# Banded attention: DRAM keeps the operands in token order alone, and the residue order is made on chip

## The reference

```python
x = x + banded_attention(layernorm(x))   # the change is here
x = x + ffn(layernorm(x))
x = x + dense_attention(layernorm(x))
x = x + ffn(layernorm(x))
```

```python
OFFSETS = sorted(set(range(0, 33)) | {48, 64, 96, 128, 192, 256, 384})
scores = stack([einsum('bhnd,bhnd->bhn', q, shift(k, delta)) for delta in OFFSETS]) * scale + pos_bias
alpha  = softmax(scores over the offsets)
out    = sum(alpha[..., i] * shift(v, delta_i))
y      = (out * sigmoid(x @ Wgate + bgate)) @ Wout + bout
```

## Time and profile before

| | us |
|---|---|
| median of 3 runs | 3871.4 (3869.67 to 3877.59) |
| the profiled execution | 3860.39 |
| its span, first to last instruction | 3858.7 |
| of it, groups of the banded attention (186.9 to 1656.6) | 1469.7 |
| TensorE busy / VectorE / ScalarE / POOL, whole span | 2995.9 / 1690.7 / 1363.9 / 494.7 |
| DMA: bytes, whole span | 419.65 MB |
| mean granted TensorE clock | 0.887 |

### The profile page before, as it was taken

The page is one execution under the profiler, slowest core; times in us unless marked ns, Lnnn a source line. Parts: engine busy times, 40 slices in busy tenths (PEclk is TensorE's granted clock), DMA queues, the critical chain, the costliest instruction groups (busy, mean ns, idle before and its releaser), DMA issues. The chain is left out here.

```text
span 3858.7 us, 99901 instructions
## 1 busy us (share of the span) xinstructions
PE 2995.9 (78%) x45340; PEld 1721.1 (45%) x45340; DVE 1690.7 (44%) x2814; ACT 1363.9 (35%) x1358; POOL 494.7 (13%) x395
## 2 busy tenths in 40 slices
PE   0466767686767676768994899989999999997898
PEld 0244545454545454543452344444444444443345
DVE  5123333333333333344044666566566666574302
ACT  0414242433342423123001454445554555554300
POOL 0101020111010111000002121111122121210000
PEclk9678888887888797879976899999999999998896
DMA  5546465645554555422923232222222222212294
GB/s 128 133 84 140 101 148 106 143 103 127 107 141 96 142 103 140 83 98 79 422 115 77 44 70 55 51 50 51 55 59 54 51 59 51 59 34 91 106 421 176
DMA packets 232389, 419.65 MB, mean 109 GB/s; under 512 B 112922, under 2 KB 141412, under 8 KB 215588
## 3 DMA queue, kind: packets, MB, share of 16 engines
q1 hardware_dynamic: 206740, 360.34, 36.5%
q10 hardware_dynamic: 25232, 52.99, 4.5%
HBM read 316.49 MB, written 94.40 MB: 106 GB/s over the span
## 5 line engine op out<-in xcount | busy, mean ns | idle before, releaser
L1353 DVE TENSOR_REDUCE b_tops<-b_slot 128x8 f32<-128x1024 f32 x576 | 680.4, 1220 | 361.6 <-PE b_slot L1210 182.5
L1390 ACT ACTIVATE b_probs<-b_slot 128x1024 f32<-128x1024 f32 x576 | 582.9, 1023 | 550.8 <-PE b_slot L1210 394.9
L1230 PE MATMUL b_outT_ps<-b_probs,b_v 128*17 128x128 f32 (+3 forms) x4608 | 318.1, 384 | 6.2 <-ACT b_probs L1390 5.5
L738 DVE TENSOR_REDUCE a_tops<-a_slot 128x16 f32<-128x1024 f32 x128 | 156.4, 1222 | 362.4 <-PE a_slot L543 361.9
L1210 PE MATMUL b_slot<-b_q_stack,b_k_stack 99*128 99x512 bf16 (+3 forms) x1280 | 274.7, 321 | 43.5 <-DVE b_tops L1353 32.8
L1210 PE MATMUL b_slot<-b_k_stack,b_q_stack 96*128 96x512 bf16 (+3 forms) x1280 | 266.8, 323 | 29.0 <-DVE b_tops L1353 20.1
L780 ACT ACTIVATE a_probs<-a_probs 128x1024 f32<-128x1024 f32 x128 | 133.4, 1053 | 349.3 <-DVE a_probs L729 335.2
L563 PE MATMUL a_slot<-a_bias_q,a_ident 128*128 128x512 bf16 x256 | 96.8, 468 | 196.4 <-DMA a_k_stack<-orders_dram 176.4
L1157 POOL TENSOR_SCALAR_AFFINE_SELECT b_probs<-b_probs 128x1024 f32<-128x1024 f32 x128 | 139.8, 1093 | 809.7 <-ACT b_probs L1390 809.7
L599 PE MATMUL a_outT_ps<-a_probs,a_v_near 128*17 128x64 f32 (+1 forms) x8448 | 147.6, 232 | 87.0 <-issue 84.2
L813 ACT ACTIVATE a_parts<-a_parts 128x1024 bf16<-128x1024 bf16 x96 | 198.1, 2063 | 28.1 <-POOL a_parts L462 14.2
(11 more groups left out here) (217 smaller groups left out, 4328.2 us busy)
## 6 DMA issues: line engine op xcount, KB each, us to landing
f_w_ring<-in_L_ffn_w_dram SPq DMA_DIRECT2D x128, 1024.0 KB, 9.4
orders_dram<-a_parts ACTq DMA_DIRECT2D x96, 512.0 KB
a_k_stack<-orders_dram SPq DMA_DIRECT2D x128, 256.0 KB, 6.7
a_q_stack<-orders_dram SPq DMA_DIRECT2D x64, 384.0 KB, 4.6
parts_dram<-b_parts SPq DMA_DIRECT2D x96, 256.0 KB
a_q_stack<-orders_dram SPq DMA_DIRECT2D x64, 256.0 KB, 5.4
a_k_stack<-orders_dram SPq DMA_DIRECT2D x128, 128.0 KB, 7.6
b_k_stack<-parts_dram SPq DMA_DIRECT2D x64, 256.0 KB, 6.7
```

The costliest lines, as they stand in the source:

```text
L738: ins = dve.tensor_reduce(tops[:, h, :, :].rearrange("p k t -> p (k t)"), src[:, :].rearrange("p (t c) -> p t c", c=64), AX.X, ALU.max)
L1230: ins = pe.matmul(outT_ps[32 * h:32 * h + HD + 1, first:last], v1[b % 2][:, j, HG * g + h, :], src[:, base + first:base + last], start=u = ...
L1353: ins = dve.tensor_reduce(out, src, AX.X, ALU.max)
L1390: act.activation(probs_of(b, g, u, h)[:, :], slot_of(step)[:, :], ACT.Exp).then_inc(taken_act, 1)
```

## The change

- The turns of the parts before the store go. The stores (now behind `part0`, `part1` and as a step `store2`, on ScalarE's queue as before) and `parts_near_dram` hold the token order alone: 256 KB each. The loads are half as large, 7 transfers as before.
- Stacks are split: `q_near`, `k_near` by token, in a ring of 4, and `q_far`, `k_far` by residue, in a ring of 3.
- A new step `turn` per pair makes the residue order from the loaded stack: VectorE for q (2 copies of 96x1024 bf16, one per head), ScalarE for k (2 as well). Both wait for the load and for `S` of the pair three back; `mx` waits for the turn of its head instead of the load.
- Schedule: in a group, loads of pair n + 4 stand behind the second `S` and of pair n + 5 behind `mrow`; the turn of pair n + 3 stands behind the second `S`, the turn of n + 4 ahead of PV. Four pairs are loaded at the start, three turned. A division now pops two steps at a time, `store2` alone.
- `mrow` writes the near and the far stack with a transfer each: 8 per group instead of 4.
- `perm` shrinks to one row of 144 columns, of which eight windows are used.

```diff
     def division(which, b, half):
-        return [(step, b, half, which) for step in ("part0", "rest1", "turn0", "part1", "part2", "turn1", "turn2")]
+        return [(step, b, half, which) for step in ("part0", "rest1", "part1", "part2", "store2")]
...
+    def turned(n):
+
+        return [("turn",) + pair_of(n)] if n < 2 * B * G else []
...
-    first += operands(0) + operands(1) + operands(2) + projection("q", 0, 1) + projection("k", 0, 1)
+    first += operands(0) + operands(1) + operands(2) + operands(3) + turned(0) + turned(1) + turned(2) + projection("q", 0, 1) + projection("k", 0, 1)
...
-            late = g in (0, 2)
-            seq += [("vin", b, g), ("S", b, g, 0)] + place[0] + top[0] + [("S", b, g, 1)] + operands(n + 3) + place[1] + top[1]
-            seq += [("S", b, g, 2)] + place[2] + [("S", b, g, 3)] + ([] if late else operands(n + 4)) + top[2] + place[3] + top[3]
-            seq += ([("fparts",) + after] if more else []) + near + place[4] + ([("fp",) + after, ("mred",) + after] if more else [])
-            seq += far[0:4] + ([("mt",) + after, ("mrow",) + after] if more else []) + (operands(n + 4) if late else [])
+            seq += [("vin", b, g), ("S", b, g, 0)] + place[0] + top[0] + [("S", b, g, 1)] + operands(n + 4) + turned(n + 3) + place[1] + top[1]
+            seq += [("S", b, g, 2)] + place[2] + [("S", b, g, 3)] + top[2] + place[3] + top[3]
+            seq += ([("fparts",) + after] if more else []) + turned(n + 4) + near + place[4] + ([("fp",) + after, ("mred",) + after] if more else [])
+            seq += far[0:4] + ([("mt",) + after, ("mrow",) + after] if more else []) + operands(n + 5)
...
-            upto = 2 if waiting[0][0] in ("part0", "part1") else 1
+            upto = 2 if waiting[0][0] != "store2" else 1
...
-def ring(b, g, pair):
-    return (2 * (b * G + g) + pair) % 3
+def ring(b, g, pair, depth):
+    return (2 * (b * G + g) + pair) % depth
...
+    BY_TOKEN, BY_RESIDUE = 4, 3
...
-        q_stack = [sb(f"q_stack{n}", [ALL_ROWS, 2, 2, N], BF16) for n in range(3)]
-        k_stack = [sb(f"k_stack{n}", [ALL_ROWS, 2, 2, N], BF16) for n in range(3)]
+        q_near = [sb(f"q_near{n}", [ALL_ROWS, 2, N], BF16) for n in range(BY_TOKEN)]
+        k_near = [sb(f"k_near{n}", [ALL_ROWS, 2, N], BF16) for n in range(BY_TOKEN)]
+        q_far = [sb(f"q_far{n}", [ALL_ROWS, 2, N], BF16) for n in range(BY_RESIDUE)]
+        k_far = [sb(f"k_far{n}", [ALL_ROWS, 2, N], BF16) for n in range(BY_RESIDUE)]
...
@@ sync
                         for part in range(PARTS):
-                            sp.wait_ge(spilled[part], 16 * count(f"turn{part}", f"turn{part}", b, g // 2, "k"))
+                            sp.wait_ge(spilled[part], 16 * count("store2", "store2", b, g // 2, "k"))
+                        if two := last_use(b, g, pair, BY_TOKEN):
+                            sp.wait_ge(filled, two)
...
                         for h in range(HG):
-                            sp.dma_start(q_stack[ring(b, g, h // 2)][QK_ROWS:ALL_ROWS, h % 2, :, :], neg_rows[PARTS * h:PARTS * (h + 1), :, :]
-                                         ).then_inc(mrows_in, 16)
+                            for order, rows in enumerate((q_near[ring(b, g, h // 2, BY_TOKEN)], q_far[ring(b, g, h // 2, BY_RESIDUE)])):
+                                sp.dma_start(rows[QK_ROWS:ALL_ROWS, h % 2, :], neg_rows[PARTS * h:PARTS * (h + 1), order, :]).then_inc(mrows_in, 16)
...
@@ tensor
-                        if h % 2 == 0:
-                            pe.wait_ge(stacked[n], STACK * count(f"stack{n}", "stack", b, g, h // 2))
+                        turns = 2 * count("turn", "turn", b, g, h // 2) - 1 + h % 2
+                        pe.wait_ge(turned_q, turns)
+                        pe.wait_ge(turned_k, turns)
...
@@ vector
+                    elif kind == "turn":
+                        _, b, g, pair = step
+                        near, far = ring(b, g, pair, BY_TOKEN), ring(b, g, pair, BY_RESIDUE)
+                        if two := last_use(b, g, pair, BY_RESIDUE):
+                            dve.wait_ge(filled, two)
+                        dve.wait_ge(stacked[near], STACK * count(f"stack{near}", "stack", b, g, pair))
+                        for h in range(2):
+                            dve.tensor_copy(q_far[far][0:QK_ROWS, h, :].rearrange("p (r a) -> p r a", r=LINKS),
+                                             q_near[near][0:QK_ROWS, h, :].rearrange("p (a r) -> p r a", r=LINKS)).then_inc(turned_q, 1)
...
@@ scalar
+                        for h in range(2):
+                            act.activation(k_far[far][0:QK_ROWS, h, :].rearrange("p (r a) -> p r a", r=LINKS),
+                                           k_near[near][0:QK_ROWS, h, :].rearrange("p (a r) -> p r a", r=LINKS), ACT.Copy).then_inc(turned_k, 1)
```

More of the change, by code:

```diff
@@ L234, in band_attention @@
     for name, kinds in {"filled": BY_DVE + BY_ACT, "taken_dve": BY_DVE, "taken_act": BY_ACT, "qk": ("q", "k"), **{kind: (kind,) for kind in (
-            "S", "PV", "ote", "z", "mred", "gmul", "fparts", "mrow", "part0", "rest1", "part1", "part2", "turn0", "turn1", "turn2", "mt", "vin", "vout")}}.items():
+            "S", "PV", "ote", "z", "mred", "gmul", "fparts", "mrow", "part0", "rest1", "part1", "part2", "store2", "turn", "mt", "vin", "vout")}}.items():
         for step in seq:
@@ L241, in band_attention @@
         if step[0] == "stack":
-            name = f"stack{ring(*step[1:])}"
+            name = f"stack{ring(*step[1:], BY_TOKEN)}"
             total[name] = nth[name, step] = total.get(name, 0) + 1
@@ L537, in products @@
                         at = 64 * i - lo
-                        pe.matmul(dst[BLK * c:BLK * (c + 1), at + first:at + last], left[rows, h, 0, BLK * blk:BLK * (blk + 1)],
-                                  right[rows, h, 0, first:last], start=start, stop=True, skip_group_check=True)
+                        pe.matmul(dst[BLK * c:BLK * (c + 1), at + first:at + last], left[0][rows, h, BLK * blk:BLK * (blk + 1)],
+                                  right[0][rows, h, first:last], start=start, stop=True, skip_group_check=True)
                     for r in range(LINKS):
@@ L542, in products, with stacks @@
                         at = 512 + 64 * pair
-                        ins = pe.matmul(dst[RES * r2:RES * (r2 + 1), at:at + 64], left[rows, h, 1, RES * r:RES * (r + 1)],
-                                        right[rows, h, 1, RES * r:RES * (r + 1)], start=start, stop=True, skip_group_check=True)
-                    return ins
+                        ins = pe.matmul(dst[RES * r2:RES * (r2 + 1), at:at + 64], left[1][rows, h, RES * r:RES * (r + 1)],
+                                        right[1][rows, h, RES * r:RES * (r + 1)], start=start, stop=True, skip_group_check=True)
+                    return ins
+                def stacks(b, g, pair):
+                    near, far = ring(b, g, pair, BY_TOKEN), ring(b, g, pair, BY_RESIDUE)
+                    return (q_near[near], q_far[far]), (k_near[near], k_far[far])
                 for step in seq:
@@ L671, in _ @@
             def _(dve):
[L673 to L675 removed]
+                for stack in k_near + k_far:
+                    dve.memset(stack[QK_ROWS:ALL_ROWS, :, :], 1.0).then_inc(cleared, 1)
+                for slot in slots:
+                    dve.memset(slot[:, :], 0.0).then_inc(cleared, 1)
                 dve.memset(outT_ps[:, :], 0.0).then_inc(cleared, 1)
@@ L774, in _, with store @@
                 act.wait_ge(cleared, N_CLEARED)
+                def store(part, b, half, which):
+                    act.wait_ge((part0_done, part1_done, part2_done)[part], count(f"part{part}", f"part{part}", b, half, which))
+                    if b >= 2:
+                        for g, pair in ((2 * half, 0), (2 * half, 1), (2 * half + 1, 0), (2 * half + 1, 1)):
+                            n = ring(b - 2, g, pair, BY_TOKEN)
+                            act.wait_ge(stacked[n], STACK * count(f"stack{n}", "stack", b - 2, g, pair))
+                    act.dma_start(scratch["parts_near"].ap()[b % 2, "qk".index(which), half, :, part], parts[:, part, :]).then_inc(spilled[part], 16)
                 for step in seq:
@@ new lines, in _ @@
+                        act.activation(parts[:, 1, :], full, ACT.Copy).then_inc(part1_done, 1)
+                        store(1, *step[1:])
+                    elif kind == "store2":
+                        store(2, *step[1:])
+                    elif kind == "turn":
+                        _, b, g, pair = step
+                        near, far = ring(b, g, pair, BY_TOKEN), ring(b, g, pair, BY_RESIDUE)
+                        if two := last_use(b, g, pair, BY_RESIDUE):
+                            act.wait_ge(filled, two)
+                        act.wait_ge(stacked[near], STACK * count(f"stack{near}", "stack", b, g, pair))
+                        for h in range(2):
```

(2 more changed lines are left out.)

82 lines of the change are left out of this document (32 added, 50 removed).

## The result

The changed kernel took 3760.8 us (median of 4 runs, 3744.7 to 3764.4) against 3874.5 for the kernel before in the same series: a ratio of 0.9688 (95%: 0.9642 to 0.9734), 114 us less. The profiled executions differ by less, 3860.4 to 3759.8, 100.6 us: that of before was quicker than the 3874.5 by 14 us, that of after than its median by 1. The trace can account for the 100.6 alone.

The account below looks back on a forecast made before the run. The banded attention was taken as a chain of hand-overs that no engine fills, with TensorE waiting for stack loads. The terms -66 + 46 + 27 - 5 - 25 - 20 gave -43 us: 3828 us from the median 3871.4, range 3768 to 3900.

Parts of the forecast that it names:

- Group 3: Seven groups 3: both load waits go, ScalarE's turn comes late; S0 to PV 33.0 to 23.3 us, 66 us saved.
- Group 2: Seven groups 2: VectorE's turn waits for the half-size load and delays fp's reduction; 6.5 us lost each, 46 in all.
- "Issue" idling and traffic: TensorE's "issue" pauses in PV, 177.5 us: halved stack traffic saves 20 us, at most some 45.
- Group 0: Seven groups 0: the load wait ahead of mx2 mostly becomes a wait for ScalarE; gain 0 to 5 us, 5 taken.
- The maximum's rows: Eight transfers instead of 4 between mt's end and S0: no gap below 8.45 us, costing 27 us over 17 groups.
- T: Time of one VectorE turn over 1024 elements of one head: 1.4 us, 128 of them, 179 us of VectorE.
- ScalarE's: ScalarE's turns: 96 fall, 128 come, 264 us of work against 198; on the path only in the groups' chains.
- Batch 0, batch 7, the small waits: 31 us of load waits without a division beside them; 25 us saved.
- Start: Before the first S0: three pairs' turns add 12.4 us, the division loses 12.4; taken at 0, bounds -10 and +10.
- B: Rival, more comes back: loads land within 5 us and the clock rises; -94 us, 3777 us, chance 0.17.
- C: Rival, slower: engines queue for absent tokens, group 2's turn over 6 us later than 35.4; +38 us, 3909, chance 0.23.
- D: Rival, no gain: load waits become equal waits for turns, POOL slowed beside VectorE's copies; -5 us, 3866, chance 0.16.

## Why the prediction was off

The side was right, and so was the mechanism in groups 3 and 0. The sum was wrong by 57 us against the profiled execution (-43 forecast, -100.6 measured). By its own steps:

- **Group 3**: forecast 33.0 to 23.3, 66 us in seven groups; measured 33.0 to 24.1, 62. The wait that was to take the load's place is there: ScalarE's turn ahead of mx2, 59.0 us in 14 places (groups 3 and 0).
- **Group 2**, the step that failed: +46 forecast, +3 measured over the seven (S0 to mt's end 39.3 us before, 39.8 after). In batch 2 the links of the chain were met: the store left at 24.8 (forecast 24.4; the working itself gives 24.8), the load 4.7 later (4), tokens 6.2 behind it (7), reduction at 37.8 (38.3). What they were laid against was wrong. I took batch 1, where S0 to mt's end was 35.8 us; batches 2 to 6 had 39.3, 44.2, 38.9, 41.1 and 40.8 before. Over the seven the reduction moved from 33.3 to 36.5 us after S0, 3.2 late and not 6.0, and from it to mt's end it took 6.1 us before and 3.3 after, so that 2.7 us were in hand and not 1.4. The hand was TensorE's own idling: in batches 4, 5 and 6 it had stopped 4.7 to 5.9 us for "issue" between reduction and mt, in batch 3 5.3 us ahead of the reduction. Batch 5, before:

```profile
1268.63 0.22 DVE L741 TENSOR_REDUCE a_far_neg<-a_slot 128x32 f32<-128x64 f32 x1 [4.46 <-PE a_slot L573]
...
1269.77 0.19 DVE L709 TENSOR_TENSOR a_neg_parts<-a_neg_max,a_neg_parts 128x32 bf16<-128x32 f32 x1
...
1274.81 1.52 PE L609 MATMUL a_outT_ps<-a_probs,a_v_far 128*17 128x32 f32 x97 [5.87 <-issue]
```

  VectorE's parts are ready at 1269.96, and mt follows at 1276.10. After, no pause in group 2 is longer than 3.1 us. So the turn does cost something, and the shorter pauses paid for it: the four batches with a long pause before became shorter by 0.3 to 3.4 us, the three without (0, 1 and 2) longer by 3.3, 4.7 and 1.3. Moving the turn away altogether gave nothing that the total shows.
- **"Issue" idling and traffic**, the other term that was too small: 20 us taken, of at most 45. The pauses in PV shrank by 24 us over the whole span, 191.0 to 166.9, about as forecast (my 177.5 leaves out what lies behind 1600 us), and the longest went from 5.9 to 3.1. Before:

```profile
PE a_outT_ps L609 <- issue: 106.8, 63, 5.9
PE a_outT_ps L599 <- issue: 84.2, 44, 5.8
```

  What had no price is the clock behind them. Group 1's PV to mt's end became 25 us shorter over seven groups, and only 13.5 of these are pauses; its S0 to PV gave 7 us more in batches 1 to 6. The stores had no price outside group 2; on top of halved loads, in the kernel before, they are worth 47 us.
- **Group 0**: 5 us of gain forecast, S0 to PV measured at 25.3 before and 25.6 after: none. With half the bytes and no turns behind the load it was 21.8. The load wait went into ScalarE's turn whole: 35 us in seven groups before, 39.5 of the 59.0 after.
- **The maximum's rows**: no gap shorter than 8.45, +27 us forecast; the shortest measured is 8.04, and the 24 gaps other than group 1's grew from 168.9 to 199.9 us, +31. The mechanism is right; the floor is 0.4 us lower than the sign that I gave, and the 27 was too low by my own rule: 21 gaps of before are shorter than 8.45, by 36 us in all (by 28 with a floor of 8.04).
- **T**: 1.4 forecast, 1.37 measured, 171 us of VectorE for 179, by luck, since the reason is another (last section). **ScalarE's** 258 us for 264: right.
- **Batch 0, batch 7, the small waits** (nine, not eight): 25 forecast; batch 0's groups 0 and 1 gave 8.7 and 14.5 us between S0 and PV, and batch 7 up to its last S0 another 6. Right in kind, a little low. **Start**: 0 forecast, 4 gained at S0; behind the band another 6 us that I had not looked for.

Of the rivals, B (-94) came nearest, but one of its two conditions did not hold: the load took 6.2 us and not 5. C's place was right and its point was not reached: VectorE's turn in group 2 began at 35.8, not beyond 41.5. D's push is real (POOL, last section) but small in the sum: VectorE's turns, POOL's delays included, cost some 16 us, which the intervals don't settle.

What remains open: how the gain from less traffic splits between earlier landings, shorter pauses and the clock, since every run that halves bytes changes all three; and the 13 us by which the medians differ more than the profiled executions.

## What to carry to other kernels

A transfer's bytes are priced in three places: its own wait, the stores that must land before it, and the engines that pause and lose their clock while it is on its way; halve each alone before trusting a sum that counts only the first. A delay is to be laid against the mean of all repetitions of its place, not against the one whose timeline was read: here one example out of seven, without the long pauses of the others, made a cost of 46 us of what was 3. And where a wait for data becomes a wait for an engine's queue, look at what stands ahead in that queue: moving one store, with the wait for POOL that it carries, behind the turn was worth more than 20 us.

## What the runs showed of the hardware that I had not expected

**TensorE's "issue" pauses end behind DMA packets of instructions.** The DMA records hold a queue q8 of the kind "instruction", with 354 packets of 16 KB in either kernel: 5.80 MB, which is 64 bytes for each of the 90,680 matmuls and weight loads, and 128 pairs of the two for each packet. In PV two pauses in a row stand 127 or 128 matmuls apart, or close to a multiple of it, where the matmuls of the next group lie between. All 107 pauses in PV before and all 106 after end 1.2 to 1.6 us after such a packet has landed. The median packet starts 0.8 us ahead of the pause; those of the nine pauses of over 3 us before started 0.75 to 3.6 us behind its beginning. Around the beginning of these nine (2 us before to 1 us after) the DMA engines' share was 0.89 on the mean, around the others 0.13. The queues in the pause of 638.5 to 643.3 us, where the packet started at 640.45 and landed at 641.90 (packets, MB, share):

```profile
q1 hardware_dynamic: 177, 0.50, 53.7%
q8 instruction: 1, 0.02, 1.9%
```

So the long pauses are TensorE waiting for its instructions, and the packets were late where loads and stores filled the DMA engines. This is read from the order in time; no run moved the one without the other.

**POOL and VectorE hold each other up while VectorE copies within SBUF.** Beside two copies of the turn, batch 2, group 2 and group 1:

```profile
627.82 4.12 POOL L467 TENSOR_TENSOR a_zb<-a_zb,a_parts 128x1024 f32<-128x1024 f32 x1 [19.29 <-ACT a_parts L831]
627.88 2.07 DVE L731 COPY a_q_far<-a_q_near 96x1024 bf16<-96x1024 bf16 x2
...
604.65 2.15 DVE L731 COPY a_q_far<-a_q_near 96x1024 bf16<-96x1024 bf16 x2
604.82 2.51 POOL L455 TENSOR_TENSOR a_spread<-a_tops,a_among 128x256 f32<-128x256 f32 x1 [41.50 <-DVE a_tops L761]
```

The subtraction takes 2.13 us alone; 2.13 and the 2.07 of the copies make 4.20, and it took 4.12. Over all 32 the spread took 1445 ns in the changed kernel and 672 with VectorE's turn cut down to 16 columns, by kind of instruction:

```profile
L455 POOL TENSOR_TENSOR a_spread<-a_tops,a_among 128x256 f32<-128x256 f32 x32 | 46.2, 1445 | 638.3 <-DVE a_tops L761 638.3
```

```profile
L457 POOL TENSOR_TENSOR a_spread<-a_tops,a_among 128x256 f32<-128x256 f32 x32 | 21.5, 672 | 635.6 <-DVE a_tops L762 635.6
```

The Trainium skill ("SBUF — State Buffer", Who interferes with whom) says that a VectorE copy in a two-port mode and a GpSimd instruction exclude each other for the whole instruction; the 4.12 us agree with it. The 39 copies with no POOL instruction beside them took 1.06 to 1.13 us for 1024 elements, the other 89 took 1.50 on the mean and up to 3.03; so the mean of 1.37 holds POOL's share, and is not the copy's own pace. The Trainium skill ("VectorE: DVE Perf Modes", Mode 2x_2P) has two results per cycle for such a copy, some 0.7 us by the estimate of the prediction; with the step of 16 elements no run here shows that rate. ScalarE needed 2.07 for the same 1024, so an undisturbed turn is cheaper on VectorE by half.

**Issuing.** The maximum's rows, small transfers within SBUF, held SP for 0.64 us each (0.74 the first), where a load from DRAM took 0.42 to 0.46 (1.25 for three, 1.83 for four).
